# Router mask spread by a transfer instead of TensorE, and eight expert buffers

## The chip, the cores and the metric

The kernel runs on one core of one Trainium2 chip. It is written instruction by instruction: every engine (PE is TensorE, DVE is VectorE, ACT is ScalarE, POOL is GpSimd, SP issues transfers) works through its own list in order, and semaphores order the lists against each other. The metric is the device time in microseconds (us) of one execution; the time of the kernel before is a median of three runs.

## What is computed

For each of 16 graphs with 512 nodes of 256 features:

```
xn = layernorm(x)
h  = relu(conv(xn, adj, W1, b1));  h = layernorm(h) * gamma + beta      # 512 x 512
x1 = x + conv(h, adj, W2, b2) + xn          # conv(v) = D^-1 H B^-1 H^T (v W^T) + b, H = (adj != 0)

x2     = layernorm(x1)
logits = x2 @ router_w + router_b           # 4 experts
mask   = softmax weights of the 2 largest logits, 0 for the other 2      # 512 x 4
s_e    = silu(x2 @ expert_w[e] + expert_b[e])     # for all 4 experts, 512 x 256 each
comb   = sum over e of mask[:, e] * s_e           # the part that the change touches
y      = x2 + comb @ out_w + out_b
out    = x1 + norm_w * y / rms(y)
```

## The kernel before

**Tiling.** The 512 nodes are four tiles (`CT`) of 128. Products are done in pieces of fp16, each as three products (`three`, lines 1025 to 1027). The experts are computed turned round: `expert_half(f, i)` gives 128 features of one expert (partitions) for all 512 nodes (free dimension), in one bank of 512 columns; `i` runs from 0 to 7, two halves to an expert. So the mask, which DVE makes with the nodes on the partitions (`mask`, 128 x 4 x 4), is needed with the nodes along the free dimension and the same on every partition.

**Steps.** `steps` calls `body` of each engine 18 times, `g` = 0 to 17. In step `g` the graph `g` is convolved (`conv`), the graph `f = g - 1` goes through router and experts (`ffn`), and the last lines of graph `g - 2` are written. 15 steps, `g` = 1 to 15, have both. Step 16 has only the experts. The order inside a step is written out by hand, for each engine.

**The mask's way before.** `make_mask` on DVE writes the mask and splits it in two fp16 parts (`m16`, lines 836 and 838). `transposed_mask` on PE turns it (line 1051, after the third of four `a3` products). `mask_copy` on ACT brings it to `mt16` (8 x 512, line 450). `mask_rows` on PE (line 1063) multiplies it for each expert with a selecting matrix `sel`, which leaves the row of that expert on all 128 partitions of a bank. `combine` on DVE (lines 743, 745) multiplies the two halves of expert `e` by that bank, and `combine_sum` (line 749) adds to `comb`: 4 multiplies and 3 sums of 128x1024.

**Around it.** In the same stretch the convolution's hidden layer is worked off: `z_part` (L753), `relu` on ACT (L454), `h_stats` (L757), the roots on POOL, `norm_h` on ACT (L458), `transposed_h` on PE (L1070), `hnt_part` on ACT (`hnth`, L463) and on DVE (`hntl`, L764), and then `v_tile` on PE (L1078 and `three`). `v_tile(g, t)` waits for `hntl` of tile `t`. `transposed_h(g, 2)` and `(g, 3)` wait for `hntl` of tile 0 and 1, whose banks they take. After `v_tile(3)` PE has `out_product`, two `incidence` products (L1102, L1103) and the front of the next step.

**Buffers.** `silu` has 4 buffers of 512 for 8 halves, so `expert` on ACT (L445) waits for `comb_st` before halves 4 to 7.

**Transfers.** SP issues in a step: `xin` of the next graph, `adjin`, `out<-x1`, `xb<-xn`, `x2o<-ob`. POOL issues the accumulating ones: `out<-yf` twice, `x2o<-x2`, `xb<-x`, `xb<-b2`.

Of the kernel before, what the change touches and what calls it, by code (L numbers as in the profile page):

```python
# [28 lines left out]
ALU = mybir.AluOpType  # L29
# [19 lines left out]
def build(nc, x, adj, wrow, w1t, b1, gamma, beta, w2t, b2, rw, rb, ew, eb, ow, ob, nw, out):  # L49
# [7 lines left out]
    with ExitStack() as ctx:  # L57
# [12 lines left out]
        MT_BANK, MB_BANK = 2, (3, 4, 3, 4)  # L70
# [38 lines left out]
        sel = sb("sel", [2 * NE, NE, P], F16)  # L109
# [70 lines left out]
        d_rdy, lg_rdy, mt_rdy = sem("d_rdy"), sem("lg_rdy"), sem("mt_rdy")  # L180
        mb_rdy = sem("mb_rdy")
# [5 lines left out]
        xs_hi, th_dn, mt_cp = sem("xs_hi"), sem("th_dn"), sem("mt_cp")  # L187
# [35 lines left out]
        def _(sp):  # L223
# [18 lines left out]
            def body(sp, g, conv, ffn, late, prep):  # L242
# [26 lines left out]
        def _(gp):  # L269
# [10 lines left out]
            nc.gpsimd.memset(sel[:, :, :], 0.0).then_inc(tables, 1)  # L280
            nc.gpsimd.memset(vbias[:, :], 0.0).then_inc(tables, 1)
            gp.wait_ge(tables, 11)
# [6 lines left out]
            for i, part in enumerate((0, NE)):  # L289
                gp.wait_ge(tables, 14 + i)  # L290
                gp.affine_select(out=sel[:, :, :], in_=sel[:, :, :], compare_op=ALU.not_equal, fill=1.0, base=-part,
                                 pattern=[[-1, NE], [0, P]], channel_multiplier=1).then_inc(tables, 1)

# [92 lines left out]
        def _(act):  # L386
# [39 lines left out]
            def setup_abs_ew():  # L426

                act.wait_ge(c_in, 16 * 6)
                af(silu[:, :, :].rearrange("p k n -> p (k n)"), flat3(ewf), ACT.Abs).then_inc(c_abs, 1)
# [18 lines left out]
            def mask_copy(act, f):  # L448
                act.wait_ge(mt_rdy, f + 1)
                af(mt16[:, :], bank[MT_BANK][0:2 * NE, 0:256].bitcast(F16), ACT.Copy).then_inc(mt_cp, 1)  # L450
# [45 lines left out]
            def body(act, g, conv, ffn, late, prep):  # L496
# [48 lines left out]
                if ffn:  # L545
                    mask_copy(act, f)
# [17 lines left out]
                if conv:  # L564
                    if not ffn:
                        hnt_part(act, g, 0)
                    norm_h(act, g, 2)
                if ffn:
                    expert(act, f, 5)
                if conv:  # L570
                    if ffn:
                        hnt_part(act, g, 0)
                    else:
# [37 lines left out]
        def _(dve):  # L611
# [58 lines left out]
            def setup_mag_a():  # L670
                dve.wait_ge(tables, 11)
# [41 lines left out]
            def setup_mag_ew():  # L713
                dve.wait_ge(c_abs, 1)
                v.reduce_max(mags[:, EX:EX + 1], silu[:, :, :].rearrange("p k n -> p (k n)"), X)
# [20 lines left out]
            def combine(f, e):  # L736

                src = silu[:, 2 * (e % 2):2 * (e % 2) + 2, :]
                m = bank[MB_BANK[e]][:, :].unsqueeze(1).to_broadcast([P, KD, C])
                dve.wait_ge(mb_rdy, 4 * f + e + 1)  # L740
                dve.wait_ge(silu_dn, 8 * f + 2 * e + 2)
                if e == 0:
                    TT(comb[:, :, :], src, m, ALU.mult).then_inc(comb_st, 1)
# [3 lines left out]
            def combine_sum(f, e):  # L747
                dve.wait_ge(comb_st, 7 * f + 2 * e)
                TT(comb[:, :, :], comb[:, :, :], silu[:, 2 * (e % 2):2 * (e % 2) + 2, :], ALU.add).then_inc(comb_st, 1)  # L749
# [55 lines left out]
            def route(f):  # L805
# [20 lines left out]
                dve.wait_ge(r_step, 9 * f + 6)  # L826
# [52 lines left out]
            def body(dve, g, conv, ffn, late, prep):  # L879
# [75 lines left out]
                if ffn:  # L955
                    combine(f, 0)
                if conv:
# [9 lines left out]
                    h_aggr(g, 3)  # L967
                if ffn:
                    combine(f, 1)
                    combine_sum(f, 1)  # L970
                if conv and ffn:
                    hnt_part(g, 0)
# [47 lines left out]
        def _(pe):  # L1020
# [26 lines left out]

            def transposed_mask(f):
                pe.wait_ge(mask_dn, f + 1)
                for t in range(CT):  # L1050
                    ins = nc.tensor.transpose(bank[MT_BANK][0:2 * NE, 0:256].bitcast(F16)[:, P * t:P * t + P],  # L1051
                                              m16[:, t, :], ident16[:, :])
                ins.then_inc(mt_rdy, 1)

            def mask_rows(f, e, g, conv):

                if e == 0:
                    pe.wait_ge(mt_cp, f + 1)
                if e < 2 and conv:
# [236 lines left out]
```

## Time and profile before

| | |
|---|---|
| median of 3 runs | 806.66 us (804.05 to 809.01) |
| the profiled execution | 805.45 us, its span 803.9 us |
| mean granted clock of PE in it | 0.969 |
| busy, share of the span | PE 91%, DVE 81%, ACT 63%, POOL 32% |
| one step in the steady part | 45.0 us |

The span goes from the first to the last instruction; 1.55 us of the execution lie outside it. A busy share is a mean over all stages. In the timeline a row is one instruction, or several of one line that are merged (x4); the products of PE overlap, so the distance from one start to the next is what a product costs there, not its duration. The clock is given as a part of full speed (1.00 is 2.4 GHz, 0.50 is 1.2 GHz).

### The profile page before, as it was taken

The numbers are of one execution on the slowest core, as the hardware profiler recorded it, in microseconds if no ns is written. First come the engines' busy times: TensorE is split into PE (matmuls) and PEld (weight loads), VectorE is DVE, ScalarE is ACT, GpSimd is POOL, SyncE is SP. The second block draws the span as 40 slices with busy tenths as digits, with TensorE's granted clock in tenths as the row PEclk, the third lists the DMA queues.
The fourth block names the chain that finished last, engine by engine and source line by source line (L and its number), as shares of the span: only waits on it lengthen the run. The fifth ranks groups of instructions, "written<-read, shape, count | busy, mean of one in ns | idle before, by whom it ended". The sixth has DMA issues, their size and how long they took to land.

```text
span 803.9 us, 16572 instructions
## 1 busy us (share of the span) xinstructions
PE 735.4 (91%) x5584; PEld 488.2 (61%) x5584; DVE 647.8 (81%) x1551; ACT 509.5 (63%) x1024; POOL 259.8 (32%) x638
## 2 busy tenths in 40 slices
PE   3537899999999999999999999999999999999782
PEld 2325467584857667584847667584848567584631
DVE  3627688888898988888898988888898989878652
ACT  4244676768575766767575766768575767766431
POOL 4031333424151424324151524324150524333211
PEclk9959899999999999999999999999999999999985
DMA  8123335535271735545271725545261825434131
GB/s 276 50 34 115 86 79 158 105 133 111 67 189 26 190 71 157 104 137 114 71 174 26 201 60 157 104 146 113 77 159 26 209 52 163 72 104 80 53 53 26
DMA packets 32264, 87.01 MB, mean 108 GB/s; under 512 B 4080, under 2 KB 4976, under 8 KB 32240
## 3 DMA queue, kind: packets, MB, share of 16 engines
q0 software_dynamic: 11520, 33.56, 25.1%
q1 hardware_dynamic: 20720, 53.14, 18.3%
q8 instruction: 14, 0.23, 0.1%
q14 instruction: 10, 0.08, 0.0%
HBM read 53.13 MB, written 16.78 MB: 87 GB/s over the span
## 4 chain that ended last, share of the span: by engine, by line
PE 85%; issue 4%; DVE 4%; ACT 3%; POOL 2%; DMA 1%; SPq 0%; POOLq 0%; ACTq 0%; DVEq 0%
PE bank L1025 17%; PE bank L1027 16%; PE bank L1026 16%; PE bank L1103 6%; PE bank L1102 6%; PE bank L1155 4%; PE bank L1070 4%; PE bank L1156 3%; PE bank L1122 3%; PE bank L1124 3%; PE bank L1063 3%; PE bank L1178 2%; PE bank L1078 1%; PE bank L1166 1%; PE bank L1051 1%
## 5 line engine op out<-in xcount | busy, mean ns | idle before, releaser
L445 ACT ACTIVATE silu<-bank,ebcol,ksc 128x512 f32<-128x512 f32 x128 | 98.8, 772 | 60.2 <-PE bank L1027 57.9
L1025 PE MATMUL bank<-xth,ewh 128*128 128x512 f16 x256 | 98.2, 384 | 1.4 <-DVE ewl L667 1.4
L376 POOL TENSOR_TENSOR yme<-yms,epsrms 128x4 f32<-128x4 f32 (+1 forms) x17 | 3.2, 189 | 296.9 <-ACT ysq L480 296.9
L1026 PE MATMUL bank<-xtl,ewh 128*128 128x512 f16 x256 | 97.8, 382 | 0.0
L1027 PE MATMUL bank<-xth,ewl 128*128 128x512 f16 x256 | 97.6, 381 | 0.0
L1026 PE MATMUL bank<-w2l,hnth 128*128 128x256 f16 x256 | 70.2, 274 | 0.0
L1025 PE MATMUL bank<-w2h,hnth 128*128 128x256 f16 x256 | 70.2, 274 | 0.0
L1027 PE MATMUL bank<-w2h,hntl 128*128 128x256 f16 x256 | 70.1, 274 | 0.0
L1155 PE MATMUL bank<-xsh,h 128*128 128x256 f16 x256 | 60.9, 285 | 4.4 <-DVE xsl L647 2.6
L458 ACT ACTIVATE hn<-r,hnb,hrs 128x512 f32<-128x512 f32 x64 | 51.4, 803 | 21.0 <-POOL hnb L319 21.0
L764 DVE SCALAR_TENSOR_TENSOR hntl<-bank,hnth 128x512 f16<-128x512 f32 x64 | 44.1, 690 | 22.0 <-ACT hnth L463 21.5
L745 DVE TENSOR_TENSOR silu<-silu,bank 128x1024 f32<-128x1024 f32 x48 | 58.4, 1216 | 4.0 <-ACT silu L445 2.6
L757 DVE BATCH_NORM_STATS2 hbn<-r 128x6 f32<-128x512 f32 x64 | 43.8, 684 | 21.9 <-ACT r L454 21.3
L1156 PE MATMUL bank<-xsl,h 128*128 128x256 f16 x256 | 60.7, 284 | 0.0
L463 ACT ACTIVATE hnth<-bank 128x512 f16<-128x512 f32 x64 | 38.0, 593 | 35.5 <-PE bank L1070 35.3
L598 ACT ACTIVATE uh<-bank,be 128x256 f16<-128x256 f32 x64 | 26.9, 470 | 52.7 <-PE bank L1103 52.7
L749 DVE TENSOR_TENSOR comb<-comb,silu 128x1024 f32<-128x1024 f32 x48 | 58.5, 1219 | 0.6
L1102 PE MATMUL bank<-uh,ht 128*128 128x256 f16 x256 | 56.8, 273 | 0.8 <-DVE ul L1007 0.8
L1102 PE MATMUL bank<-vh,h 128*128 128x256 f16 x256 | 56.8, 272 | 0.5 <-DVE vl L769 0.5
L1070 PE MATMUL bank<-ident,hn 128*128 128x128 f32 x256 | 37.8, 281 | 20.9 <-ACT hn L458 20.9
L1103 PE MATMUL bank<-vl,h 128*128 128x256 f16 x256 | 56.8, 273 | 0.0
L1103 PE MATMUL bank<-ul,ht 128*128 128x256 f16 x256 | 56.8, 273 | 0.0
(195 smaller groups left out, 2101.6 us busy)
## 6 DMA issues: line engine op xcount, KB each, us to landing
adjin<-adj SPq DMA_DIRECT2D x16, 1024.0 KB, 5.3
xin<-x SPq DMA_DIRECT2D x16, 512.0 KB, 7.0
xb<-xn SPq DMA_DIRECT2D x16, 512.0 KB, 4.8
xb<-x POOLq DMA_DIRECT2D x16, 512.0 KB, 8.7
xb<-b POOLq DMA_DIRECT2D x16, 512.0 KB, 5.4
out<-x SPq DMA_DIRECT2D x16, 512.0 KB, 4.0
x2o<-ob SPq DMA_DIRECT2D x16, 512.0 KB, 5.6
x2o<-x POOLq DMA_DIRECT2D x16, 512.0 KB, 4.6
```

The lines of the kernel that those rows point to most:

```text
L445: af(silu[:, i % 4, :], bank[E_BANK[i]][:, :], ACT.Silu, bias=ebcol[:, i:i + 1], scale=ksc[:, 2:3]).then_inc(silu_dn, 1)
L458: af(hn[:, t, :], r[:, t, :], ACT.Identity, bias=hnb[:, t:t + 1], scale=hrs[:, t:t + 1]).then_inc(hn_dn, 1)
L745: TT(src, src, m, ALU.mult).then_inc(comb_st, 1)
L749: TT(comb[:, :, :], comb[:, :, :], silu[:, 2 * (e % 2):2 * (e % 2) + 2, :], ALU.add).then_inc(comb_st, 1)
L1025: mm(outp, lh, rh, start=first, stop=False)
L1026: mm(outp, lh, rl, start=False, stop=False)
L1027: return mm(outp, ll, rh, start=False, stop=last)
L1070: ins = nc.tensor.transpose(bank[HNT_BANK[t]][:, P * k:P * k + P], hn[:, t, P * k:P * k + P], ident[:, :])
L1102: mm(b, weights[:, k, P * e:P * e + P], hi[:, k, :], start=(k == 0), stop=False)
L1103: ins = mm(b, weights[:, k, P * e:P * e + P], lo[:, k, :], start=False, stop=(k == CT - 1))
L1155: mm(b, h16[:, k, P * e:P * e + P], xsh[:, k, :], start=(k == 0), stop=False)
L1156: ins = mm(b, h16[:, k, P * e:P * e + P], xsl[:, k, :], start=False, stop=(k == CT - 1))
```

## The change

The mask is now stored by SP as one row in memory (`mrow`, 2048 floats, partition after partition), and read back by a second transfer to every one of 128 partitions (`mb`, 128 x 2048 floats, 8 KB a partition, 1 MB in all). The split in `m16`, the transposes, `mask_copy`, the four `mask_rows` and the matrix `sel` are gone. `combine` reads the mask from `mb`, where the values of one expert lie 16 floats (64 bytes) apart. There are eight buffers in `silu`, so that ACT's wait for `comb_st` is gone. Some work has another place:

- DVE: `combine(0)` stood before the statistics of the last tile, `combine(1)` and its sum before `hnt_part(0)`; all three now come behind `hnt_part(0)`.
- PE: `transposed_h(0)` now comes ahead of expert half 5, `transposed_h(1)` behind it (both stood behind it).
- ACT: `hnt_part(0)` comes ahead of `norm_h(2)` and expert half 5.
- SP: after `x2o<-ob` it waits for the mask, stores the row, waits for that, and reads it back.

```diff
-        sel = sb("sel", [2 * NE, NE, P], F16)
-        silu = sb("silu", [P, 4, 512], F32)
-        m16 = sb("m16", [P, CT, 2 * NE], F16)
-        mt16 = sb("mt16", [2 * NE, C], F16)
+        silu = sb("silu", [P, 8, 512], F32)
+        mb = sb("mb", [P, C * NE], F32)
+        mrow = nc.dram_tensor("mrow", (1, C * NE), F32).ap()
...
                     sp.dma_start(x2o[:, :, :], ob).then_inc(x2o_set, 16)
+                    sp.wait_ge(mask_dn, f + 1)
+                    sp.dma_start(mrow.rearrange("o (p m) -> (o p) m", p=P),
+                                 mask[:, :, :].rearrange("p t e -> p (t e)")).then_inc(mrow_st, 16)
+                    sp.wait_ge(mrow_st, 16 * f + 16)
+                    sp.dma_start(mb[:, :], mrow.to_broadcast([P, C * NE])).then_inc(mb_in, 16)
...
             def expert(act, f, i):
                 act.wait_ge(e_rdy, 8 * f + i + 1)
-                if i >= 4:
-
-                    act.wait_ge(comb_st, 7 * f + (1 if i < 6 else 3))
-                af(silu[:, i % 4, :], bank[E_BANK[i]][:, :], ACT.Silu, bias=ebcol[:, i:i + 1],
+                af(silu[:, i, :], bank[E_BANK[i]][:, :], ACT.Silu, bias=ebcol[:, i:i + 1],
...
             def combine(f, e):
-                src = silu[:, 2 * (e % 2):2 * (e % 2) + 2, :]
-                m = bank[MB_BANK[e]][:, :].unsqueeze(1).to_broadcast([P, KD, C])
-                dve.wait_ge(mb_rdy, 4 * f + e + 1)
+                src = silu[:, 2 * e:2 * e + 2, :].rearrange("p k (t q) -> p k t q", t=CT)
+                m = mb[:, :].rearrange("p (q t e) -> p e t q", t=CT, e=NE)[:, e].unsqueeze(1).to_broadcast([P, KD, CT, P])
+                if e == 0:
+                    dve.wait_ge(mb_in, 16 * f + 16)
                 dve.wait_ge(silu_dn, 8 * f + 2 * e + 2)
...
             def make_mask(f):
-                STT(mask[:, :, :], rank[:, :, :], 1.5, wt[:, :, :], ALU.is_lt, ALU.mult).then_inc(r_step, 1)
-                dve.wait_ge(r_step, 9 * f + 8)
-                v.tensor_copy(m16[:, :, 0:NE], mask[:, :, :]).then_inc(r_step, 1)
-                dve.wait_ge(r_step, 9 * f + 9)
-                TT(m16[:, :, NE:2 * NE], mask[:, :, :], m16[:, :, 0:NE], ALU.subtract).then_inc(mask_dn, 1)
+                STT(mask[:, :, :], rank[:, :, :], 1.5, wt[:, :, :], ALU.is_lt, ALU.mult).then_inc(mask_dn, 1)
...
-                if ffn:
-                    expert_half(f, 2)
-                    mask_rows(f, 0, g, conv)
-                    expert_half(f, 3)
-                    mask_rows(f, 1, g, conv)
-                    expert_half(f, 4)
+                if ffn:
+                    for i in range(2, 5):
+                        expert_half(f, i)
+                if conv:
+                    transposed_h(g, 0)
+                if ffn:
                     expert_half(f, 5)
-                    mask_rows(f, 2, g, conv)
-                if conv:
-                    transposed_h(g, 0)
+                if conv:
                     transposed_h(g, 1)
                 if ffn:
                     expert_half(f, 6)
-                    mask_rows(f, 3, g, conv)
                     expert_half(f, 7)
```

How the change moves DVE's list in a step of the loop, from the scaling of `dn` to the second `hntl` (after each row, the semaphores that it waits for). Before:

```order
L953 TENSOR_SCALAR dnb<-dn,ksc 128x4
L757 BN_STATS hbn<-r 128x6 [waits relu_dn]
L743 TENSOR_TENSOR comb<-silu,bank 128x1024 [waits silu_dn,mb_rdy]
L959 MEMSET spare 128x1 [waits hbn_dn]
L760 BN_AGGR hmv<-hbn 128x2
L757 BN_STATS hbn<-r 128x6 [waits relu_dn]
L966 MEMSET spare 128x1 [waits hbn_dn]
L760 BN_AGGR hmv<-hbn 128x2
L745 TENSOR_TENSOR silu<-silu,bank 128x1024 [waits silu_dn,mb_rdy]
L749 TENSOR_TENSOR comb<-comb,silu 128x1024 [waits comb_st]
L764 SCALAR_TENSOR_TENSOR hntl<-bank,hnth 128x512 [waits hnt_hi]
L745 TENSOR_TENSOR silu<-silu,bank 128x1024 [waits silu_dn,mb_rdy]
```

And with the change:

```order
L938 TENSOR_SCALAR dnb<-dn,ksc 128x4
L746 BN_STATS hbn<-r 128x6 [waits relu_dn]
L942 MEMSET spare 128x1 [waits hbn_dn]
L749 BN_AGGR hmv<-hbn 128x2
L746 BN_STATS hbn<-r 128x6 [waits relu_dn]
L949 MEMSET spare 128x1 [waits hbn_dn]
L749 BN_AGGR hmv<-hbn 128x2
L753 SCALAR_TENSOR_TENSOR hntl<-bank,hnth 128x512 [waits hnt_hi]
L732 TENSOR_TENSOR comb<-silu,mb 128x1024 [waits silu_dn,mb_in]
L734 TENSOR_TENSOR silu<-silu,mb 128x1024 [waits silu_dn]
L738 TENSOR_TENSOR comb<-comb,silu 128x1024 [waits comb_st]
L734 TENSOR_TENSOR silu<-silu,mb 128x1024 [waits silu_dn]
```

Between the first `hntl` and the second there was one instruction of 128x1024, and there are now four.

SP's list in a step of the loop, with the change (before, it ended with `x2o<-ob`):

```order
L243 DMA xin<-x 128x1024
L245 ISA [waits h_made]
L245 DMA adjin<-adj 128x4x512
L253 ISA
L254 ISA [waits x1_dn]
L254 DMA out<-x 128x1024
L257 DMA xb<-xn 128x1024 [waits xn_dn]
L260 REGISTER_ALU
L261 DMA x2o<-ob 128x1024 [waits y_dn]
L263 DMA mrow<-mask 128x16 [waits mask_dn]
L265 ISA
L266 DMA mb<-mrow 128x2048 [waits mrow_st]
```

The next `xin` is now behind two more waits.

## Rows read from the trace of the kernel before

**Rows 1.** The page: shares of the chain that ended last, by engine.
```profile
PE 85%; issue 4%; DVE 4%; ACT 3%; POOL 2%; DMA 1%; SPq 0%; POOLq 0%; ACTq 0%; DVEq 0%
```

**Rows 2.** The view by stretches; busy us and (x) counts, clock, DMA share, GB/s.
```profile
398.20:443.20 45.00, 44.89 (x351) 30.06 (x349) 39.42 (x95) 31.03 (x63) 15.70 (x39) 1.00 0.48 116
```

**Rows 3.** Timeline of PE: start, duration, line, out<-in, count, around one mask row.
```profile
417.19 0.38 PE L1026 MATMUL bank<-xtl,ewh 128*128 128x512 f16 x1
417.41 0.38 PE L1027 MATMUL bank<-xth,ewl 128*128 128x512 f16 x1
417.72 0.38 PE L1063 MATMUL bank<-mt,sel 8*128 8x512 f16 x1
418.04 0.39 PE L1025 MATMUL bank<-xth,ewh 128*128 128x512 f16 x1
```

**Rows 4.** Timeline of DVE in the same step.
```profile
412.28 0.17 DVE L834 SCALAR_TENSOR_TENSOR mask<-rank,wt 128x16 f32<-128x16 f32 x1
...
420.69 1.22 DVE L745 TENSOR_TENSOR silu<-silu,bank 128x1024 f32<-128x1024 f32 x1
421.94 1.23 DVE L749 TENSOR_TENSOR comb<-comb,silu 128x1024 f32<-128x1024 f32 x1
424.09 0.69 DVE L764 SCALAR_TENSOR_TENSOR hntl<-bank,hnth 128x512 f16<-128x512 f32 x1 [0.92 <-ACT hnth L463]
424.70 1.21 DVE L745 TENSOR_TENSOR silu<-silu,bank 128x1024 f32<-128x1024 f32 x1
425.83 0.68 DVE L764 SCALAR_TENSOR_TENSOR hntl<-bank,hnth 128x512 f16<-128x512 f32 x1
...
431.25 0.69 DVE L764 SCALAR_TENSOR_TENSOR hntl<-bank,hnth 128x512 f16<-128x512 f32 x1
```

**Rows 5.** Timeline of PE, from the first V tile to the last.
```profile
426.71 0.27 PE L1078 MATMUL bank<-vbias,ones 128*128 128x256 bf16 x1
...
428.13 0.60 PE L1070 MATMUL bank<-ident,hn 128*128 128x128 f32 x4
...
432.00 0.28 PE L1078 MATMUL bank<-vbias,ones 128*128 128x256 bf16 x1
```

**Rows 6.** Timeline of ACT in the same step.
```profile
417.83 0.78 ACT L445 ACTIVATE silu<-bank,ebcol,ksc 128x512 f32<-128x512 f32 x1 [0.86 <-PE bank L1027]
...
419.21 0.61 ACT L454 ACTIVATE r<-z 128x512 f32<-128x512 f32 x1
419.73 0.76 ACT L445 ACTIVATE silu<-bank,ebcol,ksc 128x512 f32<-128x512 f32 x1
...
423.46 0.60 ACT L463 ACTIVATE hnth<-bank 128x512 f16<-128x512 f32 x1
```

**Rows 7.** Groups of DVE instructions by form: a read of 2048 elements.
```profile
L715 DVE TENSOR_REDUCE mags<-silu 128x1 f32<-128x2048 f32 x1 | 2.3, 2286 | 1.1 <-ACT silu L429 1.1
```

**Rows 8.** DMA issues: KB of one, median us from issue to landing.
```profile
adjin<-adj SPq DMA_DIRECT2D x16, 1024.0 KB, 5.3
xin<-x SPq DMA_DIRECT2D x16, 512.0 KB, 7.0
...
out<-x SPq DMA_DIRECT2D x16, 512.0 KB, 4.0
...
vbias<-vbparts SPq DMA_DIRECT2D x3, 0.5 KB, 2.2
```

**Rows 9.** Timeline of DVE in the step without the convolution.
```profile
770.96 0.17 DVE L834 SCALAR_TENSOR_TENSOR mask<-rank,wt 128x16 f32<-128x16 f32 x1
...
783.74 1.22 DVE L749 TENSOR_TENSOR comb<-comb,silu 128x1024 f32<-128x1024 f32 x1
```

**Rows 10.** The view by stretches of 1 us, same step.
```profile
781.00:782.00 1.00, 0.56 (x3) 0.07 (x1) 0.53 (x1) 0.40 (x1) 0.00 (x0) 1.00 0.00 0
...
784.00:785.00 1.00, 0.00 (x0) 0.00 (x0) 0.96 (x1) 0.00 (x1) 0.00 (x0) 0.58 0.00 0
```

**Rows 11.** Timeline of POOL at the start.
```profile
4.01 1.40 POOL L291 TENSOR_SCALAR_AFFINE_SELECT sel<-sel 8x512 f16<-8x512 f16 x2
```

More of the change, by code:

```diff
@@ L179, in build @@
         xt_rdy, o_rdy = sem("xt_rdy"), sem("o_rdy")
-        d_rdy, lg_rdy, mt_rdy = sem("d_rdy"), sem("lg_rdy"), sem("mt_rdy")
-        mb_rdy = sem("mb_rdy")
+        d_rdy, lg_rdy = sem("d_rdy"), sem("lg_rdy")
+        mrow_st, mb_in = sem("mrow_st"), sem("mb_in")
         e_rdy = sem("e_rdy")
@@ L279, in _ @@
             nc.gpsimd.memset(ones[:, :], 1.0).then_inc(tables, 1)
-            nc.gpsimd.memset(sel[:, :, :], 0.0).then_inc(tables, 1)
             nc.gpsimd.memset(vbias[:, :], 0.0).then_inc(tables, 1)
-            gp.wait_ge(tables, 11)
+            gp.wait_ge(tables, 10)
             for m in (ident16, ident):
@@ L288, in _ @@
                              pattern=[[0, CT], [1, NE], [-1, NE]], channel_multiplier=0).then_inc(tables, 1)
[L289 to L292, printed above, removed]
             gp.wait_ge(wrow_in, 16)
@@ L428, in setup_abs_ew @@
                 act.wait_ge(c_in, 16 * 6)
-                af(silu[:, :, :].rearrange("p k n -> p (k n)"), flat3(ewf), ACT.Abs).then_inc(c_abs, 1)
+                af(silu[:, 0:4, :].rearrange("p k n -> p (k n)"), flat3(ewf), ACT.Abs).then_inc(c_abs, 1)
             def setup_abs_c():
@@ L544, in body @@
                     prep_x_hi(g + 1)
-                if ffn:
-                    mask_copy(act, f)
                 if conv and not ffn:
@@ L566, in body @@
                         hnt_part(act, g, 0)
+                    if ffn:
+                        hnt_part(act, g, 0)
                     norm_h(act, g, 2)
@@ L570, in body @@
                 if conv:
-                    if ffn:
-                        hnt_part(act, g, 0)
-                    else:
+                    if not ffn:
                         hnt_part(act, g, 1)
@@ L714, in setup_mag_ew @@
                 dve.wait_ge(c_abs, 1)
-                v.reduce_max(mags[:, EX:EX + 1], silu[:, :, :].rearrange("p k n -> p (k n)"), X)
+                v.reduce_max(mags[:, EX:EX + 1], silu[:, 0:4, :].rearrange("p k n -> p (k n)"), X)
                 for t in range(1, CT):
@@ L736, in combine @@
             def combine(f, e):
-                src = silu[:, 2 * (e % 2):2 * (e % 2) + 2, :]
-                m = bank[MB_BANK[e]][:, :].unsqueeze(1).to_broadcast([P, KD, C])
-                dve.wait_ge(mb_rdy, 4 * f + e + 1)
+                src = silu[:, 2 * e:2 * e + 2, :].rearrange("p k (t q) -> p k t q", t=CT)
+                m = mb[:, :].rearrange("p (q t e) -> p e t q", t=CT, e=NE)[:, e].unsqueeze(1).to_broadcast([P, KD, CT, P])
+                if e == 0:
+                    dve.wait_ge(mb_in, 16 * f + 16)
                 dve.wait_ge(silu_dn, 8 * f + 2 * e + 2)
                 if e == 0:
-                    TT(comb[:, :, :], src, m, ALU.mult).then_inc(comb_st, 1)
+                    TT(comb[:, :, :].rearrange("p k (t q) -> p k t q", t=CT), src, m, ALU.mult).then_inc(comb_st, 1)
                 else:
@@ L748, in combine_sum @@
                 dve.wait_ge(comb_st, 7 * f + 2 * e)
-                TT(comb[:, :, :], comb[:, :, :], silu[:, 2 * (e % 2):2 * (e % 2) + 2, :], ALU.add).then_inc(comb_st, 1)
+                TT(comb[:, :, :], comb[:, :, :], silu[:, 2 * e:2 * e + 2, :], ALU.add).then_inc(comb_st, 1)
             def z_part(g, t):
@@ L967, in body @@
                     h_aggr(g, 3)
+                if conv and ffn:
+                    hnt_part(g, 0)
                 if ffn:
+                    combine(f, 0)
                     combine(f, 1)
                     combine_sum(f, 1)
-                if conv and ffn:
-                    hnt_part(g, 0)
                 if ffn:
@@ L1046, in expert_half @@
                 ins.then_inc(e_rdy, 1)
[L1048 to L1059, printed above, removed]
-                    pe.wait_ge(z_dn, 4 * g + e + 2)
-                if e >= 2:
-                    pe.wait_ge(comb_st, 7 * f + e - 1)
-                mm(bank[MB_BANK[e]][:, :], sel[:, e, :], mt16[:, :], start=True, stop=True).then_inc(mb_rdy, 1)
             def transposed_h(g, t):
@@ L1207, in body @@
                         ins.then_inc(a3_rdy, 1)
-                        if ffn and t == 2:
-                            transposed_mask(f)
-                elif ffn:
-                    transposed_mask(f)
                 if ffn:
-                    expert_half(f, 2)
-                    mask_rows(f, 0, g, conv)
-                    expert_half(f, 3)
-                    mask_rows(f, 1, g, conv)
-                    expert_half(f, 4)
-                    expert_half(f, 5)
-                    mask_rows(f, 2, g, conv)
+                    for i in range(2, 5):
+                        expert_half(f, i)
                 if conv:
                     transposed_h(g, 0)
+                if ffn:
+                    expert_half(f, 5)
+                if conv:
                     transposed_h(g, 1)
```

26 lines of the change are left out of this document (10 added, 16 removed).

## The prediction

> **What bounds the kernel now.** I read the chain of waits first: PE holds 85% of it [rows 1]. That is a mean over stages, so the view by stretches comes next. In one whole step of the steady part (45.0 us) PE is busy for 44.89 us at a granted clock of 1.00, DVE for 39.42 [rows 2]. So PE is the bound, and whatever leaves its list in the step should shorten it, if nobody else is late. The timelines then show how close the next one is: the last V tile of PE starts at 432.00 [rows 5], and the `hntl` that it waits for starts on DVE at 431.25 and takes 0.69, so it ends at 431.94 [rows 4]. At this place DVE has no slack, while PE has no pause. Everything below turns on this stretch, from the mask (ends 412.45 [rows 4]) to the last V tile. All times are of this step; 15 steps are like it.
>
> **What the change takes from PE.** Products of 512 columns follow one another after 0.22 us (417.19 to 417.41). Across a mask row the distance is 0.63 (417.41 to 418.04), so a row costs 0.41 [rows 3]. There are four, and the four transposes of the mask open the same gap once: 5 x 0.41 = 2.07 us a step. All five lie before the first V tile, which PE can then start at 426.71 - 2.07 = 424.64; it and the transposes behind it, 1.42 and 0.60 [rows 5], are over by 426.7. If only PE counted, a step would take 42.9 us.
>
> **What it does to DVE.** The two small instructions of the split go, but behind them DVE waits for PE's products and ACT's relu in the same places as before, so the statistics of the hidden layer don't move: nothing gained. What matters is the order. Three pieces of 128x1024 (multiply 0, multiply 1, sum 1) filled DVE's list while it waited for relu and for `hnth`; now they stand behind the first `hntl`, and the waits stay empty. When can it start? On ACT the last relu (419.21) can be 0.41 earlier, since only one of PE's gaps lay before the expert half ahead of it (silu at 417.83, now 417.42): 418.80. From there silu after 0.52 (419.21 to 419.73), then a norm and another silu, 1.38 from the first silu's start (the pair silu and norm took that from 417.83 to 419.21), then 0.67, the silu's own part of that pair, until `hnth` starts: 421.37. It takes 0.60 [rows 6]. PE's transposes for it are done by then. So `hntl` 0 starts at 421.97, and DVE is free for multiply 0 at 422.6.
>
> From a start T of multiply 0 the list is fixed. A piece of 1024 costs 1.13 before something independent (424.70 to 425.83), 1.25 before the sum that needs it (420.69 to 421.94), an `hntl` 0.61 (424.09 to 424.70) [rows 4]. Multiply 0, multiply 1, sum 1, multiply 2: T + 1.13 + 1.25 + 1.13 + 1.13 = T + 4.64. Then `hntl` 1, sum 2, multiply 3, `hntl` 2, sum 3: T + 4.64 + 0.61 + 1.13 + 1.13 + 0.61 + 1.13 = T + 9.25. `hntl` 3 ends at T + 9.94. Before, it ended at 431.94. Behind it PE, ACT and DVE have the order of before, so a step changes by T - 422.0. Even at T = 422.6 that is +0.6 us: the 2.07 us of PE turn into pauses in front of V tiles 1 to 3.
>
> **The transfers.** T may also be set by `mb`. Small transfers land 2.2 us after their issue, 512 KB 4.0 when alone; `xin`, of the same size, takes 7.0 in just the place where the row is now stored, beside POOL's accumulating transfers, so their company costs 3.0 [rows 8]. The row has one packet to a partition, as `xin` has, so I charge it that too: 412.45 + 2.2 + 3.0 = 417.65. `mb` is 1 MB, as `adjin` (5.3 [rows 8]), and POOL's transfers are then nearly through: 422.95. With 0.15 for the two handovers by semaphore, an estimate, T = 423.1. The lower bound is 422.6, where the transfers hide behind `hntl` 0 (without company the data would be there at 419.95). The upper bound has company for `mb` too, another 3.0: T = 426.1. I take 423.1, since its parts are rows of the same place and size. SP holds `xin` of the next graph back by some 5 us; it is read in the next step, and costs nothing.
>
> **ACT.** `mask_copy` goes, and the wait for `comb_st`; but ACT's idle time before a silu is put down to PE [rows 6], so the eight buffers win nothing themselves. They only allow DVE to be late.
>
> **The price of a multiply.** It now reads `mb` with 64 bytes from one value to the next. The trace has no such read of this size. Nearest is the same instruction on dense operands: 1.22 from a bank, 1.23 with both operands in SBUF [rows 4]. The other end: if each value took the place of two, 1024 would cost as 2048 do, 2286 ns [rows 7], 1.07 us more. I take the near end, as the row of the same instruction.
>
> The Trainium skill speaks against that: Advanced Engine Details and Errata, section SBUF Cachelines, has lines of 16 bytes, of which each needs two hits or there is a penalty; no size is given. [...]
>
> **The sum.** The profiled execution took 805.45 us. 15 steps x (423.1 - 422.0) = +16.5. In the step without convolution the mask ends at 771.13 and the last sum at 784.96 [rows 9]; now 771.13 + 2.2 + 5.3 = 778.6 for `mb` (no company there), then 1.13 for multiply 0, three pairs of 1.25 + 1.13 and 0.10 more for the last sum to end: 787.0, +2.1. PE's expert products don't wait for the mask any more there, but the sum is what ends last. At the start POOL has the two selects for `sel` less, 1.40 us [rows 11], ahead of the roots that PE waits for; those also need the statistics of `x`, so of 0 to 1.4 I take 0.5 off. Sum: 805.45 + 16.5 + 2.1 - 0.5 = 823.6. The median of the runs is 1.2 above this execution: **825 us**, 2.2% slower. Bounds of this case: T = 422.6 gives 817, and 426.1 gives 873 (15 x 4.1, and 5.1 for the last step).
>
> **Rivals.**
> 1. *The strided read is charged.* Full price: 4 x 1.07 = 4.3 us a step on DVE's list, 15 x 5.4 + 6.4 - 0.5: 805.45 + 86.9 + 1.2 = 894. At half the price 859. For it: nothing in the list hides a longer multiply. Against: only that dense reads cost the same from either memory, which says nothing of a stride; so it gets a large chance.
> 2. *`mb` lands late*, 425 or later: each us is a us a step, 855 at 425 and 873 at 426.1. With it PE would pause for 3 us or more before V tile 1. After such a pause the granted clock falls: PE's last expert product ended in the stretch from 781, and from 784 to 785 the clock was 0.58, on its way from 2.4 to 1.2 GHz [rows 10]. In the main case the pause is 428.4 - 426.7 = 1.7 us, so I expect 1.00 to stay. The Trainium skill (TensorE: Matmul & The Clock Gate, section HAM oscillation) describes kernels that wait for transfers and start every tile cold; the trace agrees for its one long pause here.
> 3. *Faster.* PE's 2.07 us come through, since a multiply that reads no bank is shorter. To break even each would have to lose 1.1 / 4 = 0.28 us; at 0.8 us less the whole 2.07 comes: 805.45 - 31 + 2.1 - 0.5 + 1.2 = 777. Against: the sum, with no bank, takes 1.23, the multiply 1.22 [rows 4].
>
> **Chances.** Main case 0.50, strided read charged in some part 0.31, late `mb` 0.13, faster or even 0.06. About 1% (8 us, or 0.5 us a step) is what a measurement can tell from no change. Within it lie the lowest part of the main case and half of the last rival: 0.09. Faster 0.04, slower 0.87. Range: 813 (a little below T = 422.6, as DVE's start may be 0.3 better than worked out) to 897, which takes in the full charge of rival 1 and leaves out what lies above, the two charges together.
>
> **What would show it.** In the changed profile: PE busy less in a step and pauses before V tiles 1 to 3, put down to `hntl`; the last `hntl` about 1 us later after the mask than before; DVE with few pauses between `hntl` 0 and 3; `mb` landing some 10.5 us after the mask; multiplies of 1.2 us. The step would be 46.1 us. I am wrong if the multiply is not 1.2 us, if DVE waits for `mb` for more than 1 us, or if PE still fills the step.

## The result and the profile after

| | before | after |
|---|---|---|
| median, same chip | 805.36 us (803.62 to 809.01, 4 runs) | 862.89 us (861.03 to 866.23, 4 runs) |
| span of the profiled execution | 803.9 us | 859.5 us |
| mean granted clock | 0.969 | 0.929 |

The change makes the kernel slower: 1.0713 of the time before, with a 95% interval from 1.066 to 1.0766. The direction is the forecast's, the size is not (825 us); it is the first rival's "at half the price 859".

The page of the changed kernel, engines and chain, to be held against [rows 1]:

```profile
PE 731.3 (85%) x5456; PEld 500.5 (58%) x5456; DVE 681.7 (79%) x1519; ACT 496.2 (58%) x1008; POOL 241.7 (28%) x635
...
PE 54%; DVE 22%; issue 9%; ACT 9%; DMA 3%; POOL 2%; SPq 0%; POOLq 0%; ACTq 0%; DVEq 0%
```

PE's part of the chain has fallen from 85% to 54%, and DVE has risen from 4% to 22%. The groups of instructions say where: what is busy, then the mean of one in ns, then the idle time of the engine just before the group and what ended it.

```profile
L734 DVE TENSOR_TENSOR silu<-silu,mb 128x1024 f32<-128x1024 f32 x48 | 90.9, 1893 | 0.0
...
L1045 PE MATMUL bank<-vbias,ones 128*128 128x256 bf16 x64 | 20.0, 313 | 57.8 <-DVE hntl L753 56.8
...
L738 DVE TENSOR_TENSOR comb<-comb,silu 128x1024 f32<-128x1024 f32 x48 | 58.6, 1220 | 0.6
...
L732 DVE TENSOR_TENSOR comb<-silu,mb 128x1024 f32<-128x1024 f32 x16 | 30.5, 1907 | 6.7 <-DMA mb<-mrow 6.6
```

Three readings. A multiply takes 1.89 to 1.91 us where it took 1.22, while the sums beside it, dense on both sides, still take 1.22. PE waits 56.8 us for `hntl` at the first product of a V tile, where it had waited 2.9 us in the whole kernel before:

```profile
L1078 PE MATMUL bank<-vbias,ones 128*128 128x256 bf16 x64 | 17.7, 277 | 2.9 <-DVE hntl L764 2.9
```

And DVE waits for `mb` for 6.6 us in the whole kernel, 6.22 of them in the last step and 0.39 in the third, so the transfers can hardly be the reason.

One step in the timeline of DVE, from the mask to the last `hntl`, against [rows 4]:

```profile
436.87 0.17 DVE L823 SCALAR_TENSOR_TENSOR mask<-rank,wt 128x16 f32<-128x16 f32 x1
...
444.03 0.69 DVE L746 BATCH_NORM_STATS2 hbn<-r 128x6 f32<-128x512 f32 x1 [1.16 <-ACT r L444]
...
446.56 0.69 DVE L753 SCALAR_TENSOR_TENSOR hntl<-bank,hnth 128x512 f16<-128x512 f32 x1 [1.61 <-ACT hnth L453]
447.16 1.91 DVE L732 TENSOR_TENSOR comb<-silu,mb 128x1024 f32<-128x1024 f32 x1
448.99 1.91 DVE L734 TENSOR_TENSOR silu<-silu,mb 128x1024 f32<-128x1024 f32 x1
450.93 1.23 DVE L738 TENSOR_TENSOR comb<-comb,silu 128x1024 f32<-128x1024 f32 x1
452.07 1.87 DVE L734 TENSOR_TENSOR silu<-silu,mb 128x1024 f32<-128x1024 f32 x1
453.86 0.69 DVE L753 SCALAR_TENSOR_TENSOR hntl<-bank,hnth 128x512 f16<-128x512 f32 x1
...
459.13 0.69 DVE L753 SCALAR_TENSOR_TENSOR hntl<-bank,hnth 128x512 f16<-128x512 f32 x1
```

`hntl` 0 starts 9.52 us after the mask's end (437.04 to 446.56), multiply 0 10.1 us after it: both within a tenth of where the prediction put them if `mb` is not late. From there the list is full, as it said. But `hntl` 3 ends at 459.82, 12.66 us after multiply 0 began, where the prediction had T + 9.94: four longer multiplies, 2.7 us. Nothing waits for `mb` here. The queue of SP shows why (start, duration of the issue), with the DMA view of the same stretch under it:

```profile
437.07 0.33 SPq L263 DMA_DIRECT2D mrow<-mask  x1
440.62 0.33 SPq L266 DMA_DIRECT2D mb<-mrow  x1
```

```profile
mb<-mrow SPq DMA_DIRECT2D x1, 1024.0 KB, 5.9
...
mrow<-mask SPq DMA_DIRECT2D x1, 8.0 KB, 3.5
```

The row lands 3.5 us after its issue, `mb` 5.9 after its own: 446.5, 0.6 us before DVE asks for it. PE in the same step, against [rows 5]:

```profile
450.56 0.60 PE L1037 MATMUL bank<-ident,hn 128*128 128x128 f32 x4
454.60 0.39 PE L1045 MATMUL bank<-vbias,ones 128*128 128x256 bf16 x1 [3.44 <-DVE hntl L753]
...
458.20 0.42 PE L1045 MATMUL bank<-vbias,ones 128*128 128x256 bf16 x1
...
460.64 0.27 PE L1045 MATMUL bank<-vbias,ones 128*128 128x256 bf16 x1
```

And by stretches (start:end, length, busy us and count of PE, PEld, DVE, ACT, POOL, then the granted clock), against [rows 2, 10]:

```profile
423.50:472.55 49.05, 45.50 (x344) 31.49 (x341) 41.52 (x93) 30.08 (x63) 14.66 (x39) 0.93 0.48 128
452.00:453.00 1.00, 0.00 (x0) 0.00 (x0) 1.00 (x2) 0.00 (x0) 0.00 (x0) 1.00 0.00 0
453.00:454.00 1.00, 0.00 (x0) 0.00 (x0) 1.00 (x2) 0.00 (x0) 0.00 (x0) 0.73 0.00 0
...
456.00:460.00 4.00, 4.00 (x21) 2.99 (x20) 4.00 (x5) 1.55 (x3) 0.00 (x0) 0.50 0.00 0
460.00:461.00 1.00, 1.00 (x10) 0.83 (x9) 1.00 (x3) 0.75 (x2) 0.00 (x0) 0.86 0.00 0
461.00:462.00 1.00, 1.00 (x12) 0.90 (x10) 0.74 (x2) 0.00 (x0) 0.00 (x0) 1.00 0.00 0
```

PE had nothing to do from 451.2 to 454.60. In that pause the clock fell to 0.50 (1.2 GHz), and V tile 1 and the transposes behind it ran at that level: from 454.60 to 458.20 they took 3.60, where at 1.00 they took 1.42 + 0.60 [rows 5]. V tile 2 loses almost nothing by it, since its `hntl` ends only at 458.09. V tile 3 does: its `hntl` ends at 459.82, and it starts 0.8 us later, at 460.64, because PE is still busy with V tile 2 at half the clock.

The clock falls in this pause or just behind it in all 15 steps that have both parts. In most it is back before V tile 3, as in the step that begins at 582.62 (the row has the 4 us behind the start of V tile 1; from 603.62 to 604.62 the clock is 0.99):

```profile
600.42:604.42 4.00, 4.00 (x22) 3.06 (x23) 4.00 (x4) 0.41 (x1) 0.00 (x0) 0.60 0.00 0
```

Such steps take 48.3 us. Where it comes back as late as in the step above, V tile 3 is late and the step takes 49.05.

**The sum of the differences**, from one profiled execution each. The first mask starts 1.8 us earlier (95.94 against 97.74). From the first mask to the last it is 727.6 against 673.2, 54.4 more, in 15 periods: before they were nearly all 45.0, now most are 48.3 and four lie between 49.05 and 49.69. Behind the last mask it is 36.0 against 32.9, 3.0 more. -1.8 + 54.4 + 3.0 = 55.6, which is the difference of the spans. Not all of the 1.8 is kept: in the first of these periods DVE's first `z` then waits 0.93 us for PE, and V tile 0 comes 13.35 us after the mask where it comes 12.27 after it in later steps.

### The profile page after: what moved, and what is told of

Read it like the earlier page. It is cut to its first block, busy times and chain, and to the rows that moved or that the text cites. A ratio compares the mean times of both kernels' runs of the same rounds, so it can differ in the third digit from the quotient of the medians.

```text
span 859.5 us, 16132 instructions
## 1 busy us (share of the span) xinstructions
PE 731.3 (85%) x5456; PEld 500.5 (58%) x5456; DVE 681.7 (79%) x1519; ACT 496.2 (58%) x1008; POOL 241.7 (28%) x635
## 4 chain that ended last, share of the span: by engine, by line
PE 54%; DVE 22%; issue 9%; ACT 9%; DMA 3%; POOL 2%; SPq 0%; POOLq 0%; ACTq 0%; DVEq 0%
DVE silu L734 10%; PE bank L1009 9%; PE bank L1011 9%; PE bank L1010 9%; PE bank L1070 6%; PE bank L1069 6%; DVE comb L738 3%; DVE comb L732 3%; PE bank L1089 3%; PE bank L1122 3%; ACT silu L439 3%; PE bank L1091 3%; PE bank L1123 3%; DVE hntl L753 2%; ACT hn L448 2%
## 5 line engine op out<-in xcount | busy, mean ns | idle before, releaser
L734 DVE TENSOR_TENSOR silu<-silu,mb 128x1024 f32<-128x1024 f32 x48 | 90.9, 1893 | 0.0
L1011 PE MATMUL bank<-w2h,hntl 128*128 128x256 f16 x256 | 79.6, 311 | 0.0
L1009 PE MATMUL bank<-w2h,hnth 128*128 128x256 f16 x256 | 79.5, 310 | 0.0
L1010 PE MATMUL bank<-w2l,hnth 128*128 128x256 f16 x256 | 79.4, 310 | 0.0
L1045 PE MATMUL bank<-vbias,ones 128*128 128x256 bf16 x64 | 20.0, 313 | 57.8 <-DVE hntl L753 56.8
L1037 PE MATMUL bank<-ident,hn 128*128 128x128 f32 x256 | 45.5, 308 | 20.1 <-ACT hn L448 20.1
L1122 PE MATMUL bank<-xsh,h 128*128 128x256 f16 x256 | 58.5, 278 | 2.8 <-DVE xsl L635 1.0
L1123 PE MATMUL bank<-xsl,h 128*128 128x256 f16 x256 | 58.3, 277 | 0.0
L1069 PE MATMUL bank<-uh,ht 128*128 128x256 f16 x256 | 56.8, 273 | 0.8 <-DVE ul L991 0.8
L1069 PE MATMUL bank<-vh,h 128*128 128x256 f16 x256 | 56.8, 273 | 0.5 <-DVE vl L758 0.5
L1070 PE MATMUL bank<-vl,h 128*128 128x256 f16 x256 | 56.8, 273 | 0.0
```

Of the source, the lines that this page charges most:

```text
L734: TT(src, src, m, ALU.mult).then_inc(comb_st, 1)
L1009: mm(outp, lh, rh, start=first, stop=False)
L1010: mm(outp, lh, rl, start=False, stop=False)
L1011: return mm(outp, ll, rh, start=False, stop=last)
L1069: mm(b, weights[:, k, P * e:P * e + P], hi[:, k, :], start=(k == 0), stop=False)
L1070: ins = mm(b, weights[:, k, P * e:P * e + P], lo[:, k, :], start=False, stop=(k == CT - 1))
```

## The experiments

Each time is taken on the same chip as runs of the kernel before, and a ratio is to these. The kernel before took 804.6 to 805.4 us (medians) on all of them, so times of different experiments can be compared to about 1 us. The account that the experiments put to the test: the strided read costs 0.68 us a multiply, 2.7 us a step; the order adds 0.6; the transfers are hidden.

**1. Dense read.** The multiplies read 512 values side by side.

```
- m = mb[:, :].rearrange("p (q t e) -> p e t q", t=CT, e=NE)[:, e]...
+ m = mb[:, C * e:C * e + C].rearrange("p (t q) -> p t q", t=CT)...
```

> The changed kernel, but each multiply reads its 512 mask values side by side, so the values stand beside the wrong nodes. Theory A (the strided read is the term that was missed): the multiplies fall from 1.90 to 1.22 us, the four take 2.7 us less of DVE's list, PE's pause before V tile 1 falls from 3.4 to below 2 us and its clock stays at 1.00; a step is 45.6 us in place of 48.3, the kernel 815 us (808 to 822). Theory B (two operands and the wait in SBUF are what costs, not the stride): the multiplies stay near 1.9 us and the time near 863.

Measured: 815.85 us (814.36 to 817.63), 1.0122 of before (1.008 to 1.0165), 47 us below the change. The groups of DVE, and the two places where PE waits in a step:

```profile
L734 DVE TENSOR_TENSOR silu<-silu,mb 128x1024 f32<-128x1024 f32 x48 | 58.5, 1218 | 0.0
...
L732 DVE TENSOR_TENSOR comb<-silu,mb 128x1024 f32<-128x1024 f32 x16 | 19.5, 1216 | 7.0 <-DMA mb<-mrow 6.3 <-ACT silu L439 0.7
```

```profile
434.20 0.28 PE L1045 MATMUL bank<-vbias,ones 128*128 128x256 bf16 x1 [1.40 <-DVE hntl L753]
...
437.06 0.28 PE L1045 MATMUL bank<-vbias,ones 128*128 128x256 bf16 x1 [0.84 <-DVE hntl L753]
```

The steady step is 45.58 us: 0.57 above the 45.01 of before, the prediction's lower case (T = 422.6, +0.6). The rest of what a steady step has lost belongs to the stride. This is the kernel that the forecast described, and its pauses of 1.4 and 0.8 us leave the clock at 1.00.

Two periods of it are clearly longer. The first has 47.73, because DVE's first `z` waits for PE and V tile 0 starts 14.47 us after the mask, not 12.27. The third has 46.72, because `mb` is late there. It was issued at 193.23 and took 7.2 us, so it landed at 200.4, just before multiply 0 starts at 200.52. The row of the multiply names a silu, but the two halves that it needs were done at 189.9. These are rows of DVE's timeline, with the DMA view and a stretch of 1 us of the third step:

```profile
98.27 0.75 DVE L742 SCALAR_TENSOR_TENSOR z<-bank,dna,b1b 128x512 f32<-128x512 f32 x1 [2.05 <-PE bank L1011]
...
mb<-mrow SPq DMA_DIRECT2D x1, 1024.0 KB, 7.2
...
200.52 1.23 DVE L732 TENSOR_TENSOR comb<-silu,mb 128x1024 f32<-128x1024 f32 x1 [0.70 <-ACT silu L439]
...
207.00:208.00 1.00, 1.00 (x7) 0.72 (x5) 1.00 (x2) 0.00 (x0) 0.00 (x0) 0.50 0.00 0
```

PE's pause before V tile 1 was 2.19 us there, the clock fell to 0.50, and V tile 3 started 1.15 us later than in other steps.

**2. The transfers once.** Row and `mb` are transferred in the first step with experts only (the two transfers stand under the condition), so all later steps use its mask.

```
+ if not late:
...
- dve.wait_ge(mb_in, 16 * f + 16)
+ dve.wait_ge(mb_in, 16)
```

> The changed kernel, but the mask is stored and read back only in the first step with experts; later steps use that first mask again. Theory A (the two transfers are hidden behind DVE's list in all steps but the last): a step stays at 48.3 us, the last step loses the 6.2 us that DVE waits for the transfer less what the experts then hold it up, so 857 to 860 in place of 863. Theory C (1 MB a step of extra traffic slows the stretch, the late mask too): 850 or less.

Measured: 858.71 us (857.98 to 860.0), 1.0664 (1.0621 to 1.0708); the steps are still 48.3. So 1 MB of traffic a step less, and nothing gained in a steady step: the transfers were hidden. What is gained, some 4 us, is behind the last mask (32.0 us against 36.0): the wait of the last step, which has no `hntl` in front of the multiplies. In the change it looks so (against [rows 9]):

```profile
823.52 0.18 DVE L823 SCALAR_TENSOR_TENSOR mask<-rank,wt 128x16 f32<-128x16 f32 x1
829.92 1.90 DVE L732 TENSOR_TENSOR comb<-silu,mb 128x1024 f32<-128x1024 f32 x1 [6.22 <-DMA mb<-mrow]
...
839.76 1.22 DVE L738 TENSOR_TENSOR comb<-comb,silu 128x1024 f32<-128x1024 f32 x1
```

**3. PE kept at work.** 28 products of 256 columns into the half bank that V tile 1 then overwrites, in front of it; nothing uses what they compute.

```
+ if t == 1:
+     fb = bank[V_BANK[0]][:, D:2 * D]
+     for _ in range(28):
+         mm(fb, ones[:, :], vbias[:, :], start=True, stop=True)
```

> The changed kernel, with 28 products of 256 columns ahead of V tile 1 that nobody reads, in the bank that this tile then writes anew. They fill the pause of 3.4 us. Theory A (the fall of the clock costs only where V tile 1 to 3 outrun the hntl's, 0 to 0.75 us a step): the clock stays at 1.00, steps are all 48.3 us, the kernel 857 to 861. Theory E (the clock costs nothing, since DVE is late anyway): 863. If the fill is longer than the pause: above 863.

Measured: 859.42 us (858.16 to 860.55), 1.0664 (1.0621 to 1.0707). PE's pause and the view by stretches, first of this kernel:

```profile
451.94 3.22 PE L1044 MATMUL bank<-vbias,ones 128*128 128x256 bf16 x28
455.58 0.28 PE L1049 MATMUL bank<-vbias,ones 128*128 128x256 bf16 x1 [0.42 <-DVE hntl L753]
...
110.00:700.00 590.00, 562.51 (x4487) 397.29 (x4485) 508.31 (x1111) 366.87 (x752) 176.56 (x456) 1.00 0.48 129
```

then of the change:

```profile
110.00:700.00 590.00, 540.07 (x4108) 373.39 (x4106) 506.13 (x1111) 363.05 (x746) 176.01 (x456) 0.96 0.48 129
```

With the clock at 1.00 throughout, the long steps are gone: in the steady part all are 48.32 to 48.35. From the first mask to the last it is 725.7 against 727.6, 1.9 less. That is net of the fill: the first period is 1.0 longer with it (50.32 against 49.35), and the other 14 are 2.9 shorter, the 0.39 us of late `mb` in the change included. So the fallen clock costs 2 to 3 us of 56, though the mean clock of the change is 0.04 lower. DVE sets the time there, and a slow V tile 1 mostly fits into the next wait.

**4. Sums on POOL.** The dense read, and the three sums moved from DVE to POOL.

```
# DVE
- TT(comb[:, :, :], comb[:, :, :], silu[:, 2 * e:2 * e + 2, :], ALU.add)...
# POOL, after the multiply of e
+ tt(comb[:, :, :], comb[:, :, :], silu[:, 2 * e:2 * e + 2, :], ALU.add)...
```

> As the dense kernel, and the three sums of 128x1024 done by POOL, which is idle there. Theory A (DVE's list between the first and the last hntl is the bound, and takes what PE gave up): DVE gets 3.4 us of room, the pauses before V tiles 1 to 3 go, a step falls to 43 to 44 us and the kernel to 780 to 790, if a sum on POOL takes no more than 2.2 us. Theory D (something else than DVE's list holds the step at 45 us): 805 or more.

Measured: 851.89 us (849.76 to 856.21), 1.0594 (1.0543 to 1.0644). A miss by 60 us or more:

```profile
L374 POOL TENSOR_TENSOR comb<-comb,silu 128x1024 f32<-128x1024 f32 x48 | 140.5, 2928 | 53.2 <-DVE silu L740 50.1
```

```profile
L469 ACT ACTIVATE cth<-comb,ksc 128x512 f16<-128x512 f32 x32 | 21.3, 714 | 70.5 <-POOL comb L374 70.5
```

A sum takes 2.93 us on POOL against 1.22 on DVE; three in series, 8.95 us in one step, end so late that `cth` on ACT and the output products behind it wait. The idle share of an engine (POOL's 72% in the change) says nothing of how fast it is.

**5. Which distance is charged.** As the change, but the multiplies 0 to 3 read `mb` at 8, 16, 32 and 64 bytes from one value to the next.

> As the change, but the four multiplies of a step read mb at different distances from one value to the next: 8, 16, 32 and 64 bytes (the values then belong to other nodes and experts, so the output is not the reference's). It measures the price by itself. Reading 1 (the memory gives 16 bytes at a time, a value that uses only part of such a line is charged): the 8 byte multiply costs as the dense one, 1.22 us, or less than the others, and 16, 32 and 64 bytes cost the same, 1.9 us. Reading 2 (any distance is charged): all four 1.9 us. Reading 3 (the charge grows with distance): 1.2, 1.4, 1.6, 1.9 us. The step is 45.6 us plus what the four lie above 1.22.

One step:

```profile
445.46 1.22 DVE L734 TENSOR_TENSOR comb<-silu,mb 128x1024 f32<-128x1024 f32 x1
446.59 2.03 DVE L736 TENSOR_TENSOR silu<-silu,mb 128x1024 f32<-128x1024 f32 x1
448.65 1.23 DVE L740 TENSOR_TENSOR comb<-comb,silu 128x1024 f32<-128x1024 f32 x1
449.80 1.99 DVE L736 TENSOR_TENSOR silu<-silu,mb 128x1024 f32<-128x1024 f32 x1
...
453.44 1.89 DVE L736 TENSOR_TENSOR silu<-silu,mb 128x1024 f32<-128x1024 f32 x1
```

The means over the 16 steps are 1.22, 2.04, 1.99 and 1.90 us. Two floats apart costs nothing, four apart costs the full charge, and more distance adds none (it costs a little less, for a reason that stays open). That is reading 1, but for the equal cost that it expected at 16, 32 and 64 bytes. The step is 47.84 us, and 45.58 + 0 + 0.82 + 0.77 + 0.68 = 47.85: what the multiplies lie above 1.22 goes into the step to the last tenth. The kernel's time is from a single run, 857.16 us.

**6. The row turned.** A complete kernel with dense reads: PE turns the 128x16 mask with one transpose, ACT copies it to `maskt` (16x128), and the row is stored expert by expert.

```
# PE, behind a3 tile 1
+ nc.tensor.transpose(bank[2][0:NE * CT, 0:P], mask[:, :, :].rearrange("p e t -> p (e t)"), ...
# ACT
+ af(maskt[:, :], bank[2][0:NE * CT, 0:P], ACT.Copy)...
# SP
- sp.dma_start(mrow.rearrange("o (p m) -> (o p) m", p=P), ...
-              mask[:, :, :].rearrange("p t e -> p (t e)"))...
+ sp.dma_start(mrow.rearrange("o (p m) -> (o p) m", m=P), maskt[:, :])...
```

> Complete computation. The mask is turned on PE by one transpose, ACT copies the 16x128 result, and the row is stored with the nodes of one expert side by side, so that the multiplies read dense values from mb. The order is that of the change. Theory A (the 64 bytes from one value to the next cost 0.68 us a multiply, 2.7 us a step, and the rest is order): multiplies 1.22 us as in the kernel before, step 45.6 us and some 0.1 to 0.4 for the two added operations, 815 to 822 us. The row now takes a transpose and a copy more before its store, about 1 us, but only 16 packets; mb lands before hntl 0 is through. Rival B (the dense read gained only because the values were the wrong ones or the row late): nothing below 840 us.

Measured: 818.91 us (818.45 to 819.84), 1.0172 (1.014 to 1.0205). Multiplies 1.22, steps 45.69, 0.11 above experiment 1. So in a complete kernel too the dense read takes away nearly the whole difference from the change, and 44 us come back for one transpose and one copy.

**7 to 9. The order.** What is left above the kernel before, 0.6 us a step, should lie in DVE's list. Three kernels take `hntl` 1 to 3 ahead of sums and multiplies, v part 1 ahead of the ct parts on ACT, the first output product behind the first incidence product on PE, and the first `y` behind the `ul` on DVE. DVE's order in the dense ones (h `hntl`, c multiply, s sum, v `vl`, t `ctl`):

```
- h0 c0 c1 s1 c2 h1 s2 c3 h2 s3 h3 v0 t0 t1 v1
+ h0 c0 c1 h1 s1 c2 h2 s2 h3 v0 c3 v1 s3 t0 t1
```

With the mispaired dense read of experiment 1:

> The mask values are read side by side (so they belong to the wrong nodes, and the output is not the reference's), and DVE's order is another one: hntl 0, multiply 0, multiply 1, hntl 1, sum 1, multiply 2, hntl 2, sum 2, hntl 3, then v 0, multiply 3, v 1, sum 3. On ACT the v part 1 stands ahead of the ct parts, on PE the first output product behind the first incidence product. Theory A (since the change a step is as long as DVE takes from the mask to the last hntl, because three pieces of the expert results now stand behind hntl 0 and four behind it before hntl 3): with two fewer pieces of 1.2 us ahead of hntl 3 the V tile 3 starts 1.8 us earlier than in the kernel before, part of it is lost again in front of the incidence products; step about 43.9 us against 45.58 with the order of the change, 790 us in all (785 to 800). Rival B (the 2.07 us taken from PE cannot be won by any order, since the next engine in line, ACT with the norm or DVE's later work, is due at the same time): step stays at 45.0 or more, 806 to 816 us.

Measured: 793.51 us (792.93 to 794.1), 0.9855 (0.9824 to 0.9887), step 44.27.

With the turned row of experiment 6, complete:

> Complete computation: the turned row, read densely, with the order of DVE, ACT and PE in which hntl 1 to 3 stand ahead of two pieces of the expert results. Theory A: step about 44.2 us, 795 us (790 to 805), below the kernel before the change. Rival B (order cannot win PE's time): 812 to 822 us, as with the turned row alone.

Measured: **797.52 us** (795.15 to 800.65), 0.9906 (0.9872 to 0.9939). The best complete version: 0.9% faster than the kernel before, with an interval that leaves out 1, and faster than the change. By stretches, one step of it:

```profile
407.27:451.64 44.37, 43.31 (x343) 29.77 (x342) 38.44 (x92) 30.23 (x64) 14.69 (x39) 1.00 0.54 142
```

PE is the bound again, with 43.31 us of 44.37. Two waits are left on it, 0.25 us for `a1l` and this one in front of the incidence product:

```profile
428.29 0.28 PE L1085 MATMUL bank<-vh,h 128*128 128x256 f16 x1 [0.54 <-DVE vl L766]
```

With the strided read of the change, and hntl 2 and 3 still further ahead:

> Complete computation: the row and the strided read as in the change, but with DVE's order hntl 0, multiply 0, multiply 1, hntl 1, sum 1, multiply 2, hntl 2, hntl 3, v 0, sum 2, multiply 3, v 1, sum 3. Theory A (multiplies of 1.9 us on DVE's list ahead of hntl 3 are what a step is longer by, and PE has room): three pieces fewer of the list stand ahead of hntl 3, so V tile 3 starts 0.3 to 1 us earlier than in the kernel before; DVE's whole work in a step is about 42 us and does not bound; step 44.7 to 45.5, 800 to 815 us. Rival C (DVE's load as a whole is what sets the step, so that the place of a multiply does not matter): about 48 us a step, 855 to 862 us.

Measured: 827.56 us (826.12 to 829.27), 1.0282 (1.0245 to 1.032), step 46.33; above the expected range, below rival C. Order alone wins 35 us of the 57 lost, but not all, since DVE's work was pushed into the next wait:

```profile
438.23 0.28 PE L1048 MATMUL bank<-vbias,ones 128*128 128x256 bf16 x1 [0.70 <-DVE hntl L753]
442.36 0.28 PE L1072 MATMUL bank<-vh,h 128*128 128x256 f16 x1 [1.66 <-DVE vl L758]
```

The second `vl` stands behind a sum and a multiply of 1.88 us; I had counted the pieces ahead of `hntl` 3 and not those between it and `vl` 1.

**10. The order without the change.** The kernel before, its mask still on PE, with the same moves as far as its banks allow.

> The kernel before the change, with its products on PE for the mask, but with the late part of the other order (hntl 2, hntl 3, v 0 and v 1 ahead of sum 3 on DVE; v part 1 ahead of the ct parts on ACT; the first output product behind the first incidence product on PE). It asks whether the gain of the version with the turned row belongs to the order alone. Theory A (PE's list is full before the change, 44.89 us busy of 45.0, so no order can win; only with the mask off PE is there room): step 44.9 to 45.1, 802 to 809 us. Rival (the order is what gained, with or without the mask on PE): step 44.4 or less, 797 us or less.

Measured: 821.31 us (820.19 to 822.35), 1.0198 (1.0184 to 1.0212), step 46.08. Slower, which neither theory had. Two of its waits on PE over the whole kernel:

```profile
L1105 PE MATMUL bank<-vh,h 128*128 128x256 f16 x256 | 57.8, 273 | 8.7 <-DVE vl L769 8.7
...
L1125 PE MATMUL bank<-ht,a1h 128*128 128x512 f16 x128 | 48.7, 380 | 3.4 <-DVE a1l L788 3.4
```

PE had no such wait in a steady step before, so these waits, 0.54 and 0.25 us a step, are lost in full; they make 0.8 of the 1.07 by which its step is longer, the other 0.3 stays open. The same 0.54 and 0.25 stand in experiment 8. So this order costs the kernel before about 1.1 us a step, and the kernel with the mask off PE is 46.08 - 44.37 = 1.7 ahead of it. The two lists of DVE aren't the same (here multiply 3 still stands ahead of `hntl` 2), so the 1.7 is not the price of the mask's way alone. What is shown is that these moves don't gain in the kernel before, and that the change's way of the mask doesn't gain with its own order; together they come out 0.64 ahead of 45.01.

## Why the prediction was right in direction and wrong in size

**What failed: the price of the multiply.** Under "The price of a multiply" the prediction bounded it by 1.22 and 2.29 us and took the near end, "as the row of the same instruction". It is 1.90: 0.68 more, 64% of the way up in the addition. That is 2.7 us a step by the timeline, and from first mask to last 727.6 - 685.7 (experiment 1) = 41.9 us, of which 2 to 3 is the clock. The likeliest case should have been the rival. The row of the same instruction had dense operands, and what was in dispute was the stride; that row did not speak of it, as the prediction itself said a few lines below. With two ends so far apart and no row between them, the middle (859) would have been the better number. That it lies within 4 us of the measured time is in part luck: it has 0.58 us a step too little for the multiplies and 0.5 too much for the transfers. The small sum before it, 5 x 0.41 for what PE gives up, is 2.05 by the rounded figures, not 2.07, which changes nothing.

The Trainium skill was weighed there. Its rule in Advanced Engine Details and Errata, section SBUF Cachelines, is that a 16-byte line wants two hits; experiment 5 agrees: 8 bytes free, 16 bytes and more charged 0.68 to 0.82 us per 1024 output elements. Another page of the Trainium skill, VectorE: DVE Perf Modes, says in section Mode 1x that odd strides work in this mode. Nothing follows from it on their price: here a stride of 64 bytes works and takes 1.90 us in place of 1.22.

**Right: the order.** `hntl` 0 at the mask's end + 9.52, the list behind it, PE's 2.07 us turned into pauses before V tiles. The dense kernel shows the structure alone: a steady step of 45.58, against 45.01.

**Off by less: the transfers.** The row took 3.5 us, not 5.2 (company charged too high), `mb` 5.5 in the median, 5.9 in this step, not 5.3. So T was the lower bound, 422.6, and a step of the dense kernel is 0.57 longer, not 1.1. By the steady steps that would be 8.6 us instead of 16.5; measured from first mask to last it is 685.7 - 673.2 = 12.5, since the first period is 47.73 against 44.36 (the mask comes early there, and DVE then waits for PE) and the third 46.72 against 45.01 (late `mb` and a fallen clock, experiment 1). No step of the prediction spoke of either. Why `mb` takes 7.2 us in that one step stays open.

**The start and the end.** The first mask starts 1.8 us earlier, not 0.5. That the two selects' 1.40 [rows 11] came through is not shown: PE's first product starts at 9.96 in the kernel before and at 10.31 in the change, so nothing came through there; and the kernel of experiment 10, which has both selects, starts its first mask at 96.37, 1.4 earlier than the kernel before. What moves the first mask stays open. +3.0 in the last step, not +2.1: the row took only 1.4 us there (823.73 to 825.17), but `mb` landed 4.7 after it and the multiplies are longer.

**The clock.** The prediction expected 1.00 to stay in its main case, with a pause of 1.7 us, and a fall only with late `mb`. In the dense case, with 1.4 us, it stays at 1.00, but for the one step with late `mb`, where it falls after 2.19; with the 3.44 of the change it falls in all 15 steps. But its price is small, since the engine that bounds there is DVE.

**The other rivals.** Late `mb` did not come in the steady steps, where it lands 0.6 us ahead of its use; in the third step it is 0.39 us late in the change and 0.70 in the dense kernel. The buffers won nothing by themselves that a run shows; they weren't tried alone. Faster did not come in this order, and its reason, a cheaper multiply, did not show: a dense one takes 1.22 as before. With the turned row and a new order of DVE's list a step is 0.64 us shorter than before, so a part of PE's 2.07 us was there to be had.

## What to carry to other kernels

A price that no row of the trace shows is not the price of the nearest instruction: where only the access pattern is new, take a middle value or measure it first. Lay out what a vector engine reads again and again so that neighbours in the loop are neighbours in memory; here one small transpose and one copy, where the data is 128x16, saved 44 us of reading it 128x1024 at a distance. And when work leaves the engine that bounds, look at once at who stands next in the list of the other: what PE gave up turned into pauses, and a gain came out of it only with a new order on DVE.

## What the runs showed of the hardware

- DVE, operation on two f32 operands of 1024 a partition: 1.22 us with values 4 or 8 bytes apart, 2.04 at 16, 1.99 at 32, 1.90 at 64.
- POOL, an addition of this size (128x1024, f32, dense): 2.93 us in the mean of 48.
- An 8 KB row stored to memory and read back on 128 partitions: 3.5 us and 5.5 us (medians) beside other transfers; 1.4 us for the row in the last step, 6.5 in the first with experts of experiment 1, and 7.2 us for the reading in its third. The broadcast of 1 MB out of 8 KB takes what the plain load of 1 MB takes (`adjin`, 5.4).
- The granted clock fell from 1.00 to 0.50 while PE paused from 451.2 to 454.60, and came back at about 460.3, after 5.7 us of work at 0.50. In most steps of the change it came back sooner, and the same fall cost them nothing.
